# An earlier load of the query weights, a finer wait for normalised tokens, and a fifth weight buffer in the down projection of a gated attention and MLP layer

## The reference

```
xn = layernorm(x)
q, k, v = xn @ Wq.T + bq, xn @ Wk.T + bk, xn @ Wv.T + bv      # 16 heads of 128
scores  = q @ k.T / sqrt(128), causal, plus -slope[h] * |i - j|
s = softmax(scores) @ v  ->  @ Wo.T + bo
u = fwht(xn * SU_ug) / 64
h = silu(u @ W_gate.T * sg) * (u @ W_up.T * su)               # 8192 wide
d = (fwht(h * SU_dp) / 64) @ W_down.T * sd                    # fwht: Hadamard transform
out = x + s * silu(d)
```

## Time and profile before

| | us |
|---|---|
| median of the 2 runs | 4783.83 |
| the 2 runs | 4632.88 and 4934.78 |
| the profiled execution | 4636.95 |
| its span, slowest core (core 2) | 4635.4 |
| spans of the 8 cores | 4607.2 to 4635.4 |
| PE busy | 3427.8 (74%) |
| DVE busy | 1865.2 (40%) |

### The profile page before, as it was taken

The page is one execution under the profiler, slowest core; times in us unless marked ns, Lnnn a source line. Parts: engine busy times, 40 slices in busy tenths (PEclk is TensorE's granted clock), DMA queues, the critical chain, the costliest instruction groups (busy, mean ns, idle before and its releaser), DMA issues.

```text
span 4635.4 us, 61689 instructions; the slowest of 8 cores (4607.2 to 4635.4 us)
## 1 busy us (share of the span) xinstructions
PE 3427.8 (74%) x22715; PEld 1790.0 (39%) x22715; DVE 1865.2 (40%) x3576; ACT 955.5 (21%) x2347; POOL 293.5 (6%) x309
## 2 busy tenths in 40 slices
PE   0599999999924777788884929999999910625887
PEld 0366766667622322222221804444444300312333
DVE  0344444444451066666773070000000089994001
ACT  0121212212100134444452211111111510000000
POOL 0000000000000000000000001111111100100111
PEclk9999999999956877777786959999999955867999
DMA  9333232232324221111104218888888500736999
GB/s 146 29 47 51 42 54 45 47 51 42 53 26 73 61 55 37 37 37 37 37 19 71 74 15 73 77 76 76 77 77 77 55 0 0 102 52 108 178 178 163
DMA packets 633738, 296.32 MB, mean 64 GB/s; under 512 B 520675, under 2 KB 610787, under 8 KB 631267
## 3 DMA queue, kind: packets, MB, share of 16 engines
q0 software_dynamic: 422880, 191.55, 36.8%
q10 hardware_dynamic: 102912, 58.74, 4.8%
q1 hardware_dynamic: 107652, 42.10, 4.3%
HBM read 433.54 MB, written 50.33 MB: 104 GB/s over the span
## 4 chain that ended last, share of the span: by engine, by line
PE 65%; DVE 19%; DMA 5%; issue 3%; SPq 3%; another core or an unknown queue 2%; ACT 2%; DVEq 0%; ACTq 0%; POOLq 0%
PE pb L854 19%; PE pb L507 9%; PE pb L468 9%; PE pb L693 5%; PE pb L676 5%; PE pb L990 5%; PE pb L672 4%; DMA wdring<-wdT 4%; DVE C L938 3%; DVE C L940 3%; SPq L306 3%; PE pb L758 2%; PE pb L567 2%; DVE rinv L609 2%
## 5 line engine op out<-in xcount | busy, mean ns | idle before, releaser
L854 PE MATMUL pb<-xnTf,wring 128*128 128x512 bf16 x4096 | 886.5, 380 | 1.1 <-ACT xnTf L824 1.1
L990 PE MATMUL pb<-U,wdring 128*128 128x512 bf16 x2048 | 464.9, 389 | 425.5 <-DVE U L950 247.4
L705 DVE SCALAR_TENSOR_TENSOR pb<-mwin_s,slopes_l,pb 128x256 f32<-128x256 f16 x1019 | 484.5, 482 | 453.5 <-PE pb L693 434.9
L854 PEld LDWEIGHTS pb<-xnTf,wring 128*128 128x128 bf16 x4096 | 401.3, 98 | 486.4 <-issue 4.6
L715 ACT ACTIVATE ET<-pb 128x256 bf16<-128x256 f32 x1019 | 389.1, 383 | 485.9 <-DVE pb L705 392.3
L468 PE MATMUL pb<-xnT,wk_b 128*128 128x128 bf16 x8192 | 488.5, 223 | 0.2 <-ACT kstg L483 0.2
L468 PEld LDWEIGHTS pb<-xnT,wk_b 128*128 128x128 bf16 x8192 | 474.9, 100 | 10.6 <-issue 0.6
L990 PEld LDWEIGHTS pb<-U,wdring 128*128 128x128 bf16 x2048 | 201.7, 100 | 688.4 <-issue 466.2
L507 PE MATMUL pb<-wv_b,xnT 128*128 128x512 bf16 x2048 | 447.2, 379 | 0.0
L878 DVE TENSOR_TENSOR U<-A_st,B_st 128x1024 bf16<-128x1024 f32 x64 | 78.5, 1226 | 823.2 <-ACT B_st L870 823.2
L672 PE MATMUL pb<-ET,vh 128*128 128x256 bf16 x1019 | 331.1, 325 | 9.5 <-DMA vh<-v_scr 3.6
(11 more groups left out here) (85 smaller groups left out, 2525.1 us busy)
## 6 DMA issues: line engine op xcount, KB each, us to landing
wdring<-wdT POOLq DMA_DIRECT2D x128, 512.0 KB, 9.5
wring<-wupT POOLq DMA_DIRECT2D x64, 512.0 KB, 8.1
wring<-wgT POOLq DMA_DIRECT2D x64, 512.0 KB, 8.1
xTb<-xT POOLq DMA_DIRECT2D x32, 512.0 KB, 10.7
k_scr<-kstg ACTq DMA_DIRECT2D x32, 512.0 KB, 5.1
v_scr<-vstg ACTq DMA_DIRECT2D x128, 128.0 KB, 2.3
kh<-k_scr SPq DMA_DIRECT2D x16, 1024.0 KB, 7.2
vh<-v_scr SPq DMA_DIRECT2D x16, 1024.0 KB, 11.2
```

The costliest lines, as they stand in the source:

```text
L705: eng.scalar_tensor_tensor(pb[b4][:, 0:QG], mwin_s[:, coff:coff + QG], slopes_l[:, h:h + 1], pb[b4][:, 0:QG], ALU.mult, ALU.add)),
L854: ins = eng.matmul(pb[bk0 + u][:, 0:UCH], wring[slot][:, ft * 128:ft * 128 + 128], xnTf[:, ft * TOKF + u * UCH:ft * TOKF + u * UCH + UCH], ...
L990: ins = eng.matmul(pb[bk0 + e4][:, 0:FHT], wdring[slot][:, iti * 512 + e4 * 128: iti * 512 + e4 * 128 + 128], Uap(it, tk0, FHT), start=(it ...
```

## The change

It has three edits and moves no instruction to another place in any engine's list.

- The query weights: the load of `wq_b` waits for the last value product of slab 31 (`ev_cons_all[NSLAB_A - 1]`), which is the last reader of the key and value weights, where it waited for the sums of slab 39.
- The queries: half `u` waits for the slab that ends its own tokens (slab 35 for `u` = 0, slab 39 for `u` = 1), where both waited for slab 39.
- The ring of the down projection has `NWDR` = 5 buffers where it had 4 (5 x 4096 = 20480 bytes, all of region `D`), and load n waits for the matmuls of block n-5.

```diff
+    NWDR = 5 if 5 * K2 * 1024 <= szD else 4
     wdring = [at(f"wdring{i}", [128, K2 * 512], BF16, D + i * K2 * 1024)
-              for i in range(4)]
-    assert 4 * K2 * 1024 <= szD
+              for i in range(NWDR)]
+    assert NWDR * K2 * 1024 <= szD
...
     ev_wq = OP("gpsimd", lambda eng: eng.dma_start(
...
-        waits=[ev_p1_pe], dma="wqd")
+        waits=[ev_cons_all[NSLAB_A - 1]], dma="wqd")
...
+            xn_need = NSLAB_A + min(NSLAB_F, 4 * (u + 1)) - 1
             ev_qc[k2] = OP("tensor", p2_q,
-                           waits=[ev_wq, ev_xnt[NSLAB - 1],
+                           waits=[ev_wq, ev_xnt[xn_need],
                                   ev_qevac.get(k2 - 2)])
...
-                slot = gld % 4
-                prev_mm = ev_dn_mm.get(gld - 4)
+                slot = gld % NWDR
+                prev_mm = ev_dn_mm.get(gld - NWDR)
```

## The result

The changed kernel takes 0.9948 of the time of the kernel before, 95% interval 0.9929 to 0.9968: 24 us less of about 4640, with 15 to 33 us in the interval. The prediction of 4606 us is 0.9933 of its own base of 4636.95 and lies inside that interval; the shortest execution took 4606.14 us.

A forecast was written before the change was run, and what follows sets the result against it. The prediction took PE matmuls the change leaves alone as most of the time, with 95.7 us of waits as target. It summed 21 (query weights) + 0 (finer wait) + 10 (fifth buffer) = 31 us, 4636.95 to 4606 us, range 4588 to 4627.

The forecast's parts named there:

- The query weights: Ahead of the queries: load issued at 1385.3 instead of 1408.54, so PE starts them 21 us earlier.
- 2.1 us of interference: Query weight load: meeting the 512 KB token load of slab 39 makes it land about 2.1 us later.
- The finer wait: Start of the queries: waiting for slab 35 in the first half gains 0, since the weights end the wait both ways.
- What follows the queries: Stages after the queries: copies, mask load and all later work move by the same 21 us, kept to the end.
- The fifth buffer: Down projection ring: one more buffer saves 10 us, with ends of 0 and 20.7 us and some 8 more.
- the gain in the calm: Down projection: blocks land 3.1 us apart against PE's 3.45, building 2.8 us in group four, 3.9 in six and seven.
- the block loaded ahead of the six groups: Down projection: a fifth block loaded while the DMA engines are idle before the six groups saves 3.1 us.
- The 95.7 us: PE's waits for query weights (49.4 us) and down-weight blocks (46.3 us) together, 2.1% of the span, the most removable.
- the ring gives nothing: Rival, down projection: DMA engines are full throughout and waits only move, leaving the 21 us, 4616 us; chance 14%.
- The ring gives all it can: Rival, down projection: ring saves 20.7 us and some of the clock, 4595 to 4587 us in all; chance 14%.
- transfers become dearer with more blocks in flight: Rival, down projection on core 2: 0.7 us more a block over 96 blocks gives 4673 us; chance 4% (slower).
- The chances for 2%: Whole kernel: within 2% of the old time 94%, faster by over 2% 4%, slower by over 2% 2%.

The follow-up runs named there:

- the version with the queries in between: Changed kernel with query weights in four loads, the first half of the queries among the statistics of slabs 36 to 39, eight buffers: 0.9778, again 0.9775.
- half the bytes and eight buffers: Changed kernel with eight down-projection buffers and half of the down weights left out, matmuls the same: six groups 333.2 to 336.3 us.

## Why the prediction was right or wrong

- The query weights (21 us): right, and so was each step of it. The issue moved to just behind slab 39's tokens, not to the end of slab 31; the wait on PE fell by about 21 us; the run of this edit alone gives 0.9955. My 2.1 us of interference between the two loads were right for the large one (over cores 0 to 3, 52.3 us to land in the mean before, 54.6 after). The small one grew by 3 us on cores 0 and 3 (to 9.0 and 9.4) and not on 1 and 2; that stayed hidden, with 10.66 us of idle time of PE still ahead of the sums on core 3.
- The finer wait (0): right, shown by its own run. That it would begin to count once the weights came before slab 39 was right as well, and is what the version with the queries in between lives on.
- What follows the queries: right. PE's long stop for `g_st` ends 20.6 us earlier in the mean over cores 0 to 3 (4195.9, 4216.4 before), and the 21 us stay to the end.
- The fifth buffer (10 us): the mechanism was right, the size off by two, 5 us alone and 5 in the stage's time. The step that failed is the gain in the calm, 6.7 of the 10 us (2.8 in the fourth group, 3.9 in the sixth and seventh). The other term, the block loaded ahead of the six groups, 3.1 us, came out: the faster core of a pair takes 3.5 us less both with five buffers alone (378.0 to 374.5, one chip) and in the changed kernel. In place of the 6.7 us the runs show some 0.4 on these faster cores and 4 to 5 on the slower ones, which take 8.3 and 7.1 us less. The rate behind it, 3.1 us a block against PE's 3.45, was read on core 2, a slower core, and holds for one: in the changed kernel, by the same reckoning, six blocks landed on core 3 in 18.5 us (issued at 4365.23, landed after 10.2 us; issued at 4385.95, landed after 8.0), again 3.1 us each. On the faster cores, 1 and 2 there, blocks land 3.4 us apart in the calm, which is PE's own pace, so nothing is gained. Nor does a lead grow with depth: the last four groups take no less with eight buffers than with five. For some 40 us of each group the finishing transfers go beside the blocks, and blocks then land 4.3 to 5.1 us apart. The DMA share was 1.09 to 1.12 with four buffers (4220 to 4584 us, eight cores) and 1.10 to 1.11 with eight (4206 to 4558 us, cores 0 to 3), so a deeper ring found hardly any idle time of the DMA engines to fill. Where the rest of a slower core's lead is lost stays open.
- That the forecast ratio, 0.9933, still lies inside the measured interval is in part luck: the interval is 18 us wide, the first part was right, and the second came to half of its size. The 95.7 us called the most that the edits could remove leave out what shorter pauses give back in clock, some 8 us by the prediction's own later count.
- The rival "the ring gives nothing" (14%) named most of the mechanism, that waits only move (22.9 to 39.7 us of them are left with eight buffers), and its gain of 21 us is nearer to the measured 24 than the forecast's 31. "The ring gives all it can", and with it the time that follows from the Trainium skill's 358 GB/s for each core of a pair (HBM Reference, Specifications), fell: with eight buffers core 0 read and wrote about 112 MB in 384 us, 292 GB/s, and its partner as much in 365 us, 306 GB/s. That transfers become dearer with more blocks in flight is not seen: the groups took less time with each buffer more. That the bursts of a pair's cores collide, which spoke for that rival, no trace shows, since each core's times are counted from its own start.
- The chances for 2% were right: no difference in that sense.

## What to carry to other kernels

Before a ring is made deeper, compare what the stage moves with the fastest that the same queue moved over the whole stage, not over its best moments; a landing time that grows by a buffer's worth for each buffer added (medians of 9.2 to 10.9, 13.3 to 15.5 and 24 to 27 us with four, five and eight) says that depth is not the bound. Then little is gained beyond what is loaded while the consumer stands still. When a ring is spread over buffers of several names, add up the waits for all of them. When a load is moved earlier, read how far the list in front of it lets it go, and what the engine that waited for it will wait for next: here DVE's last slab was over only 14 us before the weights came, and splitting the load and its consumer, so that half of the work runs beside DVE, was worth three times the moved load.

## What was not expected of the hardware

- With four buffers, taking away the finishing loads, some 13 MB, helped more (388 to 343 us, on one chip) than taking away half of the weights (388 to 351), 48 MB; but that second kernel came close to PE's own 331 us on two cores, and its ring was too shallow on the others. Blocks of half the size took 13.8 us to land after a group's end, whole ones 15.8. Why four loads of 256 KB hold up a queue beside them for that long is open.
- In the six groups one core of each pair was slower by 7 to 27 us in all profiles with all transfers and four or more buffers, and it was each time the one that started the stage later, counted from its own start, if only by 2 to 18 us (core 0 at 4208.5 and core 1 at 4219.3: 375.6 and 393.6 us; in the changed kernel core 1 at 4198.7 and core 0 at 4201.2: 368.9 and 392.6). Without the finishing loads, or with half the bytes and eight buffers, the difference was under 5 us. That the partner's transfers are the cause is likely, and not shown.
